# Expert layers: the one-hot rows of places move from VectorE to GpSimd

## What is computed

```python
# layer 1: one expert of 32 per token, hidden size 512, and one shared expert
topk_ids = jnp.argmax(x @ gate_w, axis=-1)
order = jnp.argsort(topk_ids)
g = _grouped_mm(sorted_x, routed_gate_w, tokens_per_expert)
u = _grouped_mm(sorted_x, routed_up_w, tokens_per_expert)
d = _grouped_mm(jax.nn.silu(g) * u, routed_down_w, tokens_per_expert)
return shared_out + d[jnp.argsort(order)]
# layer 3: the four best experts of 32 per token, hidden size 128, and one shared expert
topk_scores, topk_idx = jax.lax.top_k(jax.nn.softmax(x @ router_w.T + router_bias), 4)
out = (sel * topk_scores[:, :, None]).sum(axis=1) + shared_out
```

## Time and profile before

| | |
|---|---|
| time, median of 3 runs | 4738.97 us (4735.92 to 4742.37) |
| the profiled execution: its time | 4746.18 us |
| the profiled execution: its span | 4744.5 us |
| TensorE busy | 4112.5 us (87%), 29168 instructions |
| VectorE busy | 2320.8 us (49%), 7126 instructions |
| ScalarE busy | 1780.9 us (38%), 3733 instructions |
| GpSimd busy | 953.1 us (20%), 1113 instructions |

### The profile page before, as it was taken

The page is one execution under the profiler, slowest core; times in us unless marked ns, Lnnn a source line. Parts: engine busy times, 40 slices in busy tenths (PEclk is TensorE's granted clock), DMA queues, the critical chain, the costliest instruction groups (busy, mean ns, idle before and its releaser), DMA issues. The chain is left out here.

```text
span 4744.5 us, 77442 instructions
## 1 busy us (share of the span) xinstructions
PE 4112.5 (87%) x29168; PEld 2852.5 (60%) x29168; DVE 2320.8 (49%) x7126; ACT 1780.9 (38%) x3733; POOL 953.1 (20%) x1113
## 2 busy tenths in 40 slices
PE   5999899989998999999996699996899899769986
PEld 3655655565556555655564359995566666438853
DVE  2545554555455545554543322212556666574335
ACT  3445444544554455445542111111343444313320
POOL 1212221222122212221211001111000010005557
PEclk9999999999999999999997799996899999879998
DMA  3000000000000000000000207991000000028974
GB/s 104 1 3 8 8 3 5 8 8 3 6 8 8 3 6 8 8 3 6 6 5 5 107 5 245 333 325 58 12 21 23 19 21 15 12 85 317 389 202 125
DMA packets 132637, 300.85 MB, mean 63 GB/s; under 512 B 19953, under 2 KB 86065, under 8 KB 123697
## 3 DMA queue, kind: packets, MB, share of 16 engines
q1 hardware_dynamic: 81968, 216.69, 12.8%
q0 software_dynamic: 18336, 50.09, 3.7%
q10 hardware_dynamic: 31968, 29.11, 1.8%
HBM read 245.76 MB, written 50.07 MB: 62 GB/s over the span
## 5 line engine op out<-in xcount | busy, mean ns | idle before, releaser
L487 POOL TENSOR_SCALAR a_wide_p<-a_wide_p,a_w_inv 128x512 f32<-128x512 f32 x512 | 362.7, 721 | 1553.1 <-DVE a_w_inv L1029 1552.1
L851 ACT ACTIVATE a_wide_p<-a_wide_p,a_row_min 128x512 f32<-128x512 f32 x512 | 364.1, 713 | 46.7 <-DVE a_row_min L1024 42.3
L1099 DVE TENSOR_REDUCE a_q_pad<-ring 128x4 f32<-128x1024 f32 x256 | 301.7, 1221 | 155.5 <-PE ring L679 151.7
L1024 DVE CUSTOM_DVE_ANT_0 a_wide_p<-ring,a_neg_keys 128x512 f32<-128x512 f32 x434 | 285.0, 687 | 108.9 <-PE ring L553 108.1
L553 PE MATMUL ring<-a_qk 64*128 64x512 f32 x868 | 291.7, 647 | 3.7 <-DVE a_wide_pt L1034 1.6
L899 ACT ACTIVATE a_probs<-ring 128x1024 f32<-128x1024 f32 x256 | 247.4, 1019 | 90.0 <-PE ring L693 90.0
L1446 PE MATMUL ring<-b_xgt,b_we 128*128 128x128 f32 x2016 | 235.9, 275 | 2.8 <-issue 2.3
L1446 PEld LDWEIGHTS ring<-b_xgt,b_we 128*128 128x128 f32 x2016 | 230.1, 192 | 4.1 <-issue 3.2
L2418 DVE CUSTOM_DVE_ANT_0 c_junk<-ring,c_neg_mask 128x256 f32<-128x256 f32 x512 | 182.6, 420 | 99.7 <-PE ring L1985 99.2
L583 PE MATMUL ring<-a_wide_pt,a_v 128*64 128x256 f32 x1792 | 219.8, 388 | 0.0
L679 PE MATMUL ring<-a_k_t,a_q_t 32*128 32x256 f32 x2048 | 154.2, 415 | 73.4 <-DVE a_q_pad L1099 48.9
(11 more groups left out here) (429 smaller groups left out, 8362.6 us busy)
## 6 DMA issues: line engine op xcount, KB each, us to landing
b_we<-in_experts SPq DMA_DIRECT2D x63, 1536.0 KB, 9.6
d_we<-in_experts SPq DMA_DIRECT2D x159, 384.0 KB, 6.2
d_results<-d_yb ACTq DMA_DIRECT2D x159, 128.0 KB, 6.1
b_results<-b_yb ACTq DMA_DIRECT2D x63, 128.0 KB, 9.3
x_all<-in_x SPq DMA_DIRECT2D x1, 4096.0 KB, 14.1
a_cb<-in_ctx SPq DMA_DIRECT2D x16, 256.0 KB, 2.7
b_turned<-a_heads_t SPq DMA_DIRECT2D x16, 256.0 KB, 2.4
b_rows<-a_heads SPq DMA_DIRECT2D x16, 256.0 KB, 2.1
```

The source lines that it names most:

```text
L487: ins = pool.tensor_scalar(wide_p[:, h % 4, t, :], wide_p[:, h % 4, t, :], w_inv[:, t, h:h + 1], 1.0, ALU.mult, ALU.mult)
L851: ins = act.activation(wide_p[:, h % 4, t, :], wide_p[:, h % 4, t, :], ACT.Exp, scale=-1.0, bias=row_min[:, h, t:t + 1], accum_out=row_sum ...
L1024: dve.tensor_tensor_reduce(wide_p[:, h % 4, t, :], wbank(name), neg_keys[w % 2][:], -0.125, 3.0e38, ALU.add, ALU.min, row_min[:, h, t:t + ...
L1099: dve.tensor_reduce(q_pad[:, :, 2 * i:2 * i + 2, HD].rearrange("p t h -> p h t"), s, AX.X, ALU.max, negate=True).then_inc(nr.taken(name), 1)
```

## The change

GpSimd makes the `by_place` rows of all chunks, in the same order and into the same buffers; VectorE makes the `by_block` rows alone. Two semaphores are new: `parts_ready`, by which VectorE tells GpSimd that `partf` is there (it takes the place of a link of VectorE with itself), and `places_made`, by which GpSimd tells TensorE of each chunk. TensorE now waits for both halves of a chunk. GpSimd's instruction compares as VectorE's did, and adds 0.0 as a second operation.

```diff
@@ def _(pool) @@
                         pool.memset(scan_ones[:], 1.0).then_inc(consts, 1)
+                        pool.wait_ge(parts_ready, 1)
+                        for c in range(chunks):
+                            if c >= 2:
+                                pool.wait_ge(pairs_used, c - 1)
+                            for i in range(PAIR):
+                                k, t = (PAIR * c + i) // T, (PAIR * c + i) % T
+                                ins = pool.tensor_scalar(by_place[:, c % 2, i, :], count16[:, 0:P], partf[:, 0, k, t:t + 1], 0.0,
+                                                         ALU.is_equal, ALU.add)
+                            ins.then_inc(places_made, 1)
                         ac.wait_taken(pool, ("inverse",))
@@ def find_tokens(c) @@
                             name = ("inverse",)
+                            pe.wait_ge(places_made, c + 1)
                             pe.wait_ge(pairs_made, c + 1)
@@ def places() @@
-                            link(dve.tensor_copy(partf[:], slot_parts[:]))
+                            dve.tensor_copy(partf[:], slot_parts[:]).then_inc(parts_ready, 1)
+                            dve.wait_ge(parts_ready, 1)
@@ def make_pairs(c) @@
                                 k, t = (PAIR * c + i) // T, (PAIR * c + i) % T
-                                dve.tensor_scalar(by_place[:, c % 2, i, :], count16[:, 0:P], partf[:, 0, k, t:t + 1], None, ALU.is_equal)
                                 ins = dve.tensor_scalar(by_block[:, c % 2, i, :], count16[:, 0:NB], partf[:, 1, k, t:t + 1], token[:, t:t + 1],
                                                         ALU.is_equal, ALU.mult)
```

More of the change, by code:

```diff
@@ L1324, in expert_layer @@
                     linked = sem(ctx, f"{tag}_linked")
+                    parts_ready = sem(ctx, f"{tag}_parts_ready")
+                    places_made = sem(ctx, f"{tag}_places_made")
                     pairs_made = sem(ctx, f"{tag}_pairs_made")
```

## The result

The changed kernel takes 4773.76 us, the median of 4 runs (4764.42 to 4782.98); the kernel before, run beside it on the same chip, took 4737.44. The ratio is 1.0072, with a 95% interval of 1.0054 to 1.009: slower by some 34 us by the ratio (the two medians lie 36 apart), where 11 us less were forecast, and outside the range of 4719 to 4757.

The account below looks back on a forecast made before the run. VectorE's one-hot rows were taken to bound stage D's routing, TensorE stage B's. Terms -3.8 (B) and -7.3 (D) sum to -11.1 us: 4727.9 from 4738.97, own range 4723 to 4730, 8-in-10 range 4719 to 4757.

Parts of the forecast that it names:

- s: Stage D: interval between two rows of places on GpSimd, taken as 0.35 us from a multiplication's time and memset's slope.
- The upper bound: Stage D: largest interval allowed between GpSimd's rows of places, 0.67 us, as if four times fewer columns saved nothing.
- The rival of a slow compare: Stage D: GpSimd's compare alone is slow, interval 0.52 to 0.67 us; at 0.67 the kernel takes 4767.5; chance 0.11.
- The formula: Stage D: last pair ready at 4219.5 + 128 s + 7 x 0.138 / s, 4267.1 instead of 4274.4, so -7.3 us.
- Turns between the engines: Stage D: VectorE goes at GpSimd's pace while both run, one row of blocks every 0.35 us, not every 0.23.
- the 0.03 forecast: Stage D: GpSimd loses 0.03 us or less to each VectorE turn, so nothing was added to its row interval.
- The rival of whole instructions in turn: Stage D: each row of places waits out a whole row-of-blocks interval, 0.35 + 0.23 = 0.58 us; total 4756.2; chance 0.12.
- Quick GpSimd: Stage D: rows of places 0.27 us apart, TensorE then the bound; -19.5 us in all, 4719.5; chance 0.12.
- The gain eaten: Stage D: second operation costs like the first, interval 0.46 us, total 4741.3; chance 0.31 together with TensorE's clock.
- TensorE's clock: Stage D: low clock in each shared-expert part makes a cycle 6.5 us, gives back 3.5, total 4731.4; within the joint 0.31.
- -3.8: Stage B: TensorE's four waits for chunk ends disappear because GpSimd makes rows of places ahead, saving 3.8 us.
- the experts follow the index one for one: Stage D: whatever ends earlier in the routing ends the kernel earlier by as much, everything behind following in order.

Follow-up runs that it names:

- the kernel with quick rows: Changed kernel, but stage D's GpSimd rows multiply by the column, then by zero (output wrong): 4848.51 against 4743.37 us for the kernel before, ratio 1.0223.
- the second run of forms: Kernel before, with idle GpSimd making spare rows by pairs of operations: multiply, multiply and multiply, add took 371 to 380 ns, other pairs 712 to 776; no total given.

## Why the prediction was wrong

**The step that failed** is the size of one term, s, the interval of GpSimd's rows of places: 0.35 was taken and 0.705 measured, over the 128 rows of stage D. "692 - 384 x 0.83 = 373 ns at 128 columns" took a multiplication's time and memset's slope. The value for the multiplication was right (371 measured), and so was memset's slope for it (0.76 to 0.87 measured, for 0.83); the step from it to a compare was wrong. I had called L487 "the same operation with the same kind of scalar column", and written elsewhere that it does one operation per element where this does two. Both were wrong: it does two multiplications, which is one of the pairs that GpSimd has a quick way for. The upper bound, 0.67 "as if four times fewer columns saved nothing", is no bound either across that divide: 0.705 lies above it, and 256 columns of compare take 1.190.

**What the trace of before could have told.** It held no GpSimd instruction with a column operand other than L487's sort, so the slow way was not to be read from it. That GpSimd's time hangs on the operation was: a power of two tiles takes it 5.4 us for 32 columns there, in stage A.

```profile
L507 POOL TENSOR_TENSOR rstd<-base,minus_half 128x32 f32<-128x32 f32 x16 | 87.0, 5437 | 9.2 <-DVE base L1065 9.2
```

The rival of a slow compare (0.11, up to s = 0.67 and 4767.5) had nearly the size: a slow row, whatever its neighbour. It is what happened, though the compare as such is not to blame (a multiplication alone takes as long), and the range was cut short of it.

**The formula held.** With s = 0.70 it gives 4219.5 + 128 x 0.70 + 7 x 0.138 / 0.70 = 4310.5 for the last pair, 36.1 later than before; the token index is 35.9 later in its stage. (The last term, 1.4 us for the products, has no counterpart here: GpSimd never stopped.) With quick rows it gave -7.3, and -6.5 was measured. With six of eight rows the index came 14.5 later.

**Turns between the engines.** For quick rows of the change's own width the step was right: in the kernel with quick rows VectorE made its rows of blocks 0.35 apart where it makes them 0.23 apart alone, one to each of GpSimd's. It is not a rule of one instruction to one. In the second run of forms two of VectorE's instructions, a pair, went to each multiplication of 256 columns (pairs start at 4227.38, 4227.86, 4228.33, thus 0.475 apart, where a pair alone takes 0.394), and beside the multiplications of 128 columns that followed the pairs kept their 0.39. The forecast of that run, 0.45 us for VectorE's rows beside all sixteen, was wrong. Beside the 256 columns:

```profile
4226.88 2.43 POOL L1392 TENSOR_SCALAR d_try<-d_count,d_partf 128x256 f32<-128x256 f32 x5 [13.43 <-DVE d_partf L1575]
...
4227.38 0.24 DVE L1589 TENSOR_SCALAR d_by_place<-d_count,d_partf 128x128 f16<-128x128 f16 x1
4227.55 0.40 DVE L1590 TENSOR_SCALAR d_by_block<-d_count,d_partf,d_token 128x159 f16<-128x159 f16 x1
...
4228.33 0.24 DVE L1589 TENSOR_SCALAR d_by_place<-d_count,d_partf 128x128 f16<-128x128 f16 x1
```

For the slow rows that the change really has it was wrong, in a way that costs nothing: VectorE's rows of blocks start 4.08 / 16 = 0.255 apart beside them, hardly more than the 0.23 alone, and not one every 0.71. GpSimd loses more to it than the 0.03 forecast. These are its first six rows in stage D, with VectorE at work beside them, and the four from 4219.60, with VectorE idle but for the first 0.1 us:

```profile
4215.11 4.51 POOL L1373 TENSOR_SCALAR d_by_place<-d_count,d_partf 128x128 f16<-128x128 f16 x6 [13.42 <-DVE d_partf L1547]
...
4219.60 2.78 POOL L1373 TENSOR_SCALAR d_by_place<-d_count,d_partf 128x128 f16<-128x128 f16 x4
```

The first six are 0.75 apart, (4219.60 - 4215.11) / 6, the four 0.69, (2.78 - 0.71) / 3. VectorE has its rows made early and is idle for long (busy 22 of the 50 us from 4250), so the mean stays at 0.705. The rival of whole instructions in turn fell: 0.06 is lost and not 0.23. (The Trainium skill, SBUF — State Buffer, section on the two separate sides, has the loser of the shared ports fully blocked; the quick rows agree, with 0.35 for VectorE's 0.23, and the rows of places of this change don't show it, with 0.255 for 0.23.)

**The other rivals.** Quick GpSimd needed an interval of 0.27, which no form with a column reached. The gain eaten put a second operation at the price of the first; a compare alone takes 0.594 and with the addition 0.717, so the second costs 0.12, close to the 0.11 assumed. The greater part of the excess is not the second operation: the compare alone stands 0.22 above the 0.371 of the quick pair. (The Trainium skill, GPSIMD Engine Reference, section on pitfalls for Q7 kernels, gives 2.03 cycles per element plain and 1.03 unrolled. The slow rows take some 3.5 ns a column, about twice the first of these at 1.2 GHz; the trace doesn't agree.) TensorE's clock was never what decided, since TensorE waited in every cycle; but its last sums, granted 0.85 and not 1.00, took 16.42 us and not 13.86, 2.6 more.

**Stage B and what follows.** -3.8 was forecast and -5.3 came in the changed kernel's profile, -6.0 in the kernel with this part alone: the waits went as described, and what is beyond them the prediction had no term for. That the experts follow the index one for one held within 3 us: 35.9 later at the index, 38.2 at the first block, 35.3 at the last result. Summed over the profile, -4.4 up to the start of stage D, +35.3 in it and -1.1 behind it make the 29.8 us of the two spans.

## What to carry to other kernels

Before work goes to GpSimd, find or make a row with the very pair of operations; a neighbour that differs only in the operation can be off by a factor of two, and an estimate from width or type does not show it. Where a slower engine is to help, give it the share that ends together with the other engine's: here half the rows gained 8 to 13 us, and all of them cost 34. In the stage where another engine is the bound and the helper can work ahead, the same slow rows cost nothing.

## What the hardware showed that was not expected

- The speed of GpSimd's operations with a column depends on the pair of operations: at 128 columns 371 to 380 ns for multiply, multiply and multiply, add, and 594 to 625 for a compare or a multiplication alone and 709 to 776 for pairs beginning with a compare, subtraction or addition. One multiplication is slower (598) than two (371).
- GpSimd's products of two tiles (429 ns in f16, 460 in f32, 128 columns, beside VectorE's work) and its copy (290) are quicker than a compare with a number (670).
- Beside GpSimd's quick rows of 128 columns VectorE's rows of blocks start 0.35 us apart, one to each, and alone 0.23; beside the compare's rows 0.25, and these go from 0.69 to 0.75.
- Experts whose gathers all read one row took 402 us and not 284, with weights and results landing 3 to 4 us later too (one kernel).
